# Second attention of a two-block model: a new order of the unit on every engine, and who scales which score pairs

## What is computed

```python
def xattn1(latents, context, Wq, Wk, Wv, Wo, q_norm_w, k_norm_w):
    kv = concatenate([context, latents], axis=1)          # 64 + 256 keys a batch
    q = (latents @ Wq)  # 32 heads of 128
    k, v = kv @ Wk, kv @ Wv                               # 8 key/value heads of 128
    q, k = rms_norm(q, q_norm_w), rms_norm(k, k_norm_w)
    probs = softmax(einsum(q, k) / sqrt(128))             # 4 query heads share a kv head
    return einsum(probs, v) @ Wo
x = x + tanh(g_xattn[1]) * xattn1(layernorm(x), ctx, ...)
```

## Time and profile before

| | us |
|---|---|
| median of 3 runs | 1468.65 (1466.71 to 1475.12) |
| the profiled execution | 1468.23, its span 1466.4 |
| PE busy | 1393.1 (95%) |
| DVE busy | 1056.6 (72%) |
| ACT busy | 799.1 (54%) |
| POOL busy | 464.6 (32%) |
| mean granted TensorE clock | 0.992 of full speed |

### The profile page before, as it was taken

How to read it: one execution, slowest core, us unless ns; L and a number is a source line. 1 busy time by engine, 2 the same in 40 slices (tenths; PEclk the granted TensorE clock), 3 DMA queues, 4 the chain that set the end, 5 groups by cost and what they waited for, 6 DMA issues and landing times.

```text
span 1466.4 us, 24308 instructions
## 1 busy us (share of the span) xinstructions
PE 1393.1 (95%) x7976; PEld 1197.5 (82%) x7976; DVE 1056.6 (72%) x2794; ACT 799.1 (54%) x2210; POOL 464.6 (32%) x591
## 2 busy tenths in 40 slices
PE   4999999999999988999999999999999999999988
PEld 4899999987778877888888888888888888887777
DVE  7777777887514347787787787777787787787775
ACT  4778777773202225565555555555655655555631
POOL 3965555655937421111121111111111211112220
PEclk9999999999999999999999999999999999999999
DMA  5221111212312201001001001001001001010001
GB/s 194 73 72 60 57 70 72 72 58 72 104 42 72 98 1 72 1 1 73 1 1 72 0 1 72 0 1 72 0 1 72 0 1 72 14 42 1 1 8 51
DMA packets 14959, 63.96 MB, mean 44 GB/s; under 512 B 1761, under 2 KB 1761, under 8 KB 10657
## 3 DMA queue, kind: packets, MB, share of 16 engines
q1 hardware_dynamic: 14880, 63.07, 12.3%
HBM read 60.97 MB, written 2.10 MB: 43 GB/s over the span
## 4 chain that ended last, share of the span: by engine, by line
PE 40%; DVE 15%; issue 5%; ACT 4%; DVEq 0%; ACTq 0%
PE psum L57 12%; PE psum L59 11%; PE psum L58 11%; PE psum L1359 2%; PE psum L1453 2%; DVE mx L1044 2%; DVE pT_hi L1017 2%; DVE w1o_lo L1006 1%; DVE pT_lo L1013 1%; DVE p L1059 1%; DVE w1q_lo L1006 1%; ACT pT_hi L1215 1%; DVE dump L1037 1%; DVE oT_lo L1023 1%; DVE v_lo L1074 1%
## 5 line engine op out<-in xcount | busy, mean ns | idle before, releaser
L1292 ACT ACTIVATE p<-psum,nb,rq 128x320 f32<-128x320 f32 x256 | 155.1, 613 | 163.1 <-DVE nb L1048 163.0
L57 PE MATMUL psum<-w1q_hi,xnT_lo 128*128 128x512 f32 x288 | 121.9, 423 | 16.4 <-DVE v_lo L1068 8.6
L981 POOL TENSOR_TENSOR rk<-ssk,rms_eps 128x3 f32<-128x3 f32 x32 | 6.3, 196 | 352.1 <-DVE ssk L1085 352.1
L1013 DVE TENSOR_TENSOR pT_lo<-psum,pT_hi 128x512 fp32r<-128x512 f32 x128 | 88.1, 689 | 40.0 <-ACT pT_hi L1215 38.3
L59 PE MATMUL psum<-w1q_hi,xnT_hi 128*128 128x512 f32 x288 | 114.5, 398 | 0.0
L58 PE MATMUL psum<-w1q_lo,xnT_hi 128*128 128x512 f32 x288 | 113.7, 395 | 0.0
L1044 DVE TENSOR_REDUCE mx<-psum 128x2 f32<-128x640 f32 x128 | 105.0, 820 | 6.5 <-PE psum L59 0.9
L1256 ACT ACTIVATE q_raw<-psum 128x512 f32<-128x512 f32 x64 | 38.2, 597 | 122.7 <-PE psum L59 122.7
L57 PE MATMUL psum<-w1o_hi,oT_lo 128*128 128x512 f32 x256 | 100.5, 393 | 0.0
L58 PE MATMUL psum<-w1o_lo,oT_hi 128*128 128x512 f32 x256 | 100.3, 392 | 0.0
L59 PE MATMUL psum<-w1o_hi,oT_hi 128*128 128x512 f32 x256 | 99.8, 390 | 0.0
(11 more groups left out here) (236 smaller groups left out, 4658.3 us busy)
## 6 DMA issues: line engine op xcount, KB each, us to landing
raw_q<-in_w0q SPq DMA_DIRECT2D x8, 1024.0 KB, 4.9
raw_o<-in_w0o SPq DMA_DIRECT2D x8, 1024.0 KB, 4.8
raw_q<-in_w1q SPq DMA_DIRECT2D x8, 1024.0 KB, 7.5
raw_o<-in_w1o SPq DMA_DIRECT2D x8, 1024.0 KB, 4.8
raw_kv<-in_w_gu SPq DMA_DIRECT2D x10, 512.0 KB, 3.6
raw_gu<-in_w_gu SPq DMA_DIRECT2D x10, 512.0 KB, 3.6
raw_kv<-in_w0kv SPq DMA_DIRECT2D x8, 515.0 KB, 3.3
raw_kv<-in_w1kv SPq DMA_DIRECT2D x8, 512.0 KB, 5.5
```

The costliest lines, as they stand in the source:

```text
L57: pe.matmul(out, w[1], m[0], start=start, stop=False)
L1013: last = dve.tensor_tensor(k.pT[1][:, kt, 2 * hp:2 * hp + 2, :], bank.rearrange("p (h q) -> p h q", h=2), f(k.pT[0][:, kt, 2 * hp:2 * hp + ...
L1292: last = act.activation(k.p1[:, tile, h, :], s_pair(j)[:, h % 2, :], ACT.Exp, bias=k.nb[:, i:i + 1], scale=k.rq[:, i:i + 1], accum_out=k.r ...
```

## The change

All of it is in the second attention and in the first steps of the tail.

- The unit is put in another order on PE, ACT and DVE. Turns 0, 1 and 2 of a unit's p come at the end of the unit itself (around its last scores); turns 3, 4 and 5, p_v and out stay in the next unit, spread between its projections: p_v(0) and turns 3 and 4 behind kv, then half of q's projection, k's transposes, turn 5, the other half, q's first transposes, p_v(1), q's second transposes, and scores and out as before.
- q is projected by pairs of heads instead of by tiles of tokens: 48 matmuls of 256 columns instead of 24 of 512. Its transposes and its split go by pairs of heads too, and score pairs 2 and 3 change places, so that the first two pairs use the first half of q.
- POOL scales the second and the third score pair; DVE the first and the fourth (before: POOL the first, DVE the other three).
- The next group's weight pieces are split elsewhere: o's in batch 1; kv's and q's in batch 3, q's last two low parts in the next group's first unit.
- DVE's list of the 8 groups is written out; PE, ACT and POOL keep the loop.

```diff
-    PAIRS = [(0, 0), (0, 1), (1, 0), (1, 1)]
+    PAIRS = [(0, 0), (1, 0), (0, 1), (1, 1)]
...
+        order = ["t3", "t4", "k", "t5", "q0", "q1", "t0", "t1", "t2"]
...
+    def pieces(g, b):
+
+        return {1: [("o", g, i) for i in range(CONV["o"])],
+                3: [("kv", g + 1, i) for i in range(CONV["kv"])] + [("q", g + 1, i) for i in range(CONV["q"])]}.get(b, [])
...
-                    p_scale(n, 0)
+                    p_scale(n, 1)
+                    p_scale(n, 2)
...
-                if j == 0:
+                if j in (1, 2):
                     return
...
+                    if prev:
+                        t_lo(u, b, 5)
+                    q_squares(n, 0)
+                    if conv:
+                        w_lo(*conv[1])
+                    q_squares(n, 1)
+                    q_lo(n, b, 0)
+                    for c in conv[2:4]:
+                        w_lo(*c)
+                    if prev:
+                        pv_lo(u, b, 1)
+                    q_lo(n, b, 1)
                     row_max(n, 0)
                     row_max(n, 1)
...
                     scale_p(n, 0)
+                    scale_p(n, 1)
+                    row_max(n, 2)
                     if prev:
+                        x_add(u, b, 0)
+                    scale_p(n, 2)
+                    if prev:
+                        x_add(u, b, 1)
+                    t_lo(n, b, 0)
+                    row_max(n, 3)
+                    t_lo(n, b, 1)
...
+                    t_lo(n, b, 2)
                     scale_p(n, 3)
...
-            loop(dve, body, tail)
+            for g in range(NKV):
+                body(g, g == 0, g < NKV - 1)
+            tail(NKV * BATCH)
...
+            def q_proj(n, b, hp):
+                for tile in range(2):
+                    t = 2 * b + tile
+                    for c in range(CH):
+                        last = mm3(pe, y_bank(b, "q", hp)[:, tile * 256:(tile + 1) * 256],
+                                   [w[:, c, t * PART:(t + 1) * PART] for w in k.xnT],
+                                   [w[:, c, hp * 256:(hp + 1) * 256] for w in k.w_q], c == 0, c == CH - 1)
+                last.then_inc(q_full, 1)
...
+                    if prev:
+                        if b % 2 == 0:
+                            pe.wait_ge(kv_split, n + 1)
+                        p_v(u, b, 0)
+                        before = ln_tiles(u)
+                        turn(u, b, 3, late=before[1] if before else False)
+                        turn(u, b, 4)
...
+                    if b % 2 == 0:
+                        pe.wait_ge(cx_split, 2 * g + b // 2 + 1)
+                    else:
+                        pe.wait_ge(kv_split, n + 1)
+                    q_proj(n, b, 0)
                     if prev:
-                        turn(n, b, 4)
-                        turn(n, b, 5)
-                        p_v(n, b, 0)
-                        pe.wait_ge(t_split, 6 * (n - 1) + 5)
+                        pe.wait_ge(t_split, 6 * u + 4)
                     pe.wait_ge(k_scaled, n + 1)
...
+                    if prev:
+                        turn(u, b, 5)
+                        pe.wait_ge(pv_split, 2 * u + 1)
+                    else:
+                        pe.wait_ge(kv_split, n + 1)
+                    q_proj(n, b, 1)
+                    pe.wait_ge(kt_split, n + 1)
+                    q_turn(n, b, 0)
+                    if prev:
+                        p_v(u, b, 1)
+                    q_turn(n, b, 1)
                     scores(n, b, 0)
                     scores(n, b, 1)
...
                     scores(n, b, 2)
                     if prev:
-                        out(n, b, 1)
+                        out(u, b, 1)
+                    turn(n, b, 0)
+                    turn(n, b, 1)
                     scores(n, b, 3)
+                    for i, tile in enumerate(late):
+                        pe.wait_ge(t_split, 6 * n + i + 1)
+                        ln.pe_turn(pe, *tile, ln_bank(b, i))
+                    turn(n, b, 2, late=late[0] if late else False)
 
             def tail(n):
+                u = n - 1
                 ffn1.pe_ag(pe, 0)
+                pe.wait_ge(x_added, 2 * u - 1)
+                p_v(u, 0, 0)
+                turn(u, 0, 3, late=ln_tiles(u)[1])
+                turn(u, 0, 4)
+                ffn1.pe_ag(pe, 1)
                 ffn1.pe_base(pe, 0)
...
```

More of the change, by code:

```diff
@@ L1069, in body @@
                                       ALU.subtract).then_inc(kv_split, 1)
+                    if b == 0 and not first:
+                        w_lo("q", g, 2)
+                        w_lo("q", g, 3)
                     if b % 2 == 0:
@@ L1087, in body @@
                     last.then_inc(ssk_ready, 1)
+                    if prev:
+                        t_lo(u, b, 3)
+                        t_lo(u, b, 4)
+                    dve.wait_ge(rk_ready, n + 1)
+                    for i in range(nk):
+                        last = dve.tensor_scalar(k.k_raw[:, i, :], k.k_raw[:, i, :], k.rk[:, i:i + 1], None, ALU.mult)
+                    last.then_inc(k_scaled, 1)
+                    if prev:
+                        pv_lo(u, b, 0)
                     if not nxt and b >= 2:
@@ new lines, in body @@
+                    if prev:
+                        t_evac(u, b, 5)
+                    if conv:
+                        w_hi(*conv[1])
+                    for late in ln_tiles(n):
+                        ln.act_norm(act, *late)
+                    q_copy(n, b, 1)
+                    q_hi(n, b, 0)
+                    for c in conv[2:4]:
+                        w_hi(*c)
+                    if prev:
+                        pv_evac(u, b, 1)
+                    q_hi(n, b, 1)
+                    exps(n, 0)
@@ L1300, in tail @@
+                    exps(n, 1)
+                    for c in conv[4:]:
+                        w_hi(*c)
+                    exps(n, 2)
+                    t_evac(n, b, 0)
+                    t_evac(n, b, 1)
+                    for i, tile in enumerate(ln_tiles(n)):
+                        ln.act_hi(act, *tile, ln_bank(b, i))
+                    t_evac(n, b, 2)
+                    exps(n, 3)
             def tail(n):
+                u = n - 1
                 ffn1.act_ag(act, 0)
+                pv_evac(u, 0, 0)
@@ L1362, in turn, with p_v @@
                 last.then_inc(t_full, 1)
-            def p_v(n, b, hp, alone=False):
+            def p_v(u, b, hp):
                 pb = (b - 1) % BATCH
-                pe.wait_ge(t_split, 6 * (n - 1) + 3 * (hp + 1))
-                if not alone:
-                    pe.wait_ge(q_copied, 2 * n + hp + 1)
+                pe.wait_ge(t_split, 6 * u + 3 * (hp + 1))
                 for kt in range(2):
@@ L1375, in p_v, with out @@
                 last.then_inc(pv_full, 1)
-            def out(n, b, j):
-                pe.wait_ge(pv_split, 2 * n)
+            def out(u, b, j):
                 for h in range(GH):
+                    if j == 0 and h % 2 == 0:
+                        pe.wait_ge(pv_split, 2 * u + h // 2 + 1)
                     last = mm3(pe, y_bank(b, "d", j)[:, :], [w[:, h, j * PART:(j + 1) * PART] for w in k.oT],
@@ L1382, in out, with q_turn @@
                 last.then_inc(d_full, 1)
+            def q_proj(n, b, hp):
[6 more added lines that the diff above has]
+                last.then_inc(q_full, 1)
+            def q_turn(n, b, hp):
+                pe.wait_ge(q_copied, 2 * n + hp + 1)
+                for hh in range(2):
+                    for tile in range(2):
+                        at = tile * 256 + hh * HD
+                        last = pe.transpose(x_bank(b, "q", hp)[:, (2 * hh + tile) * PART:(2 * hh + tile + 1) * PART],
+                                            k.q_raw[:, hp, at:at + HD], k.ident[:, :])
+                last.then_inc(qt_full, 1)
             def scores(n, b, j):
                 tile, hp = PAIRS[j]
-                if j == 0:
-                    pe.wait_ge(kt_split, n + 1)
-                if hp == 0:
-                    pe.wait_ge(qt_split, 2 * n + tile + 1)
+                if tile == 0:
+                    pe.wait_ge(qt_split, 2 * n + hp + 1)
                 if not (isinstance(n, int) and 4 * n + j < 2):
@@ L1399, in body @@
                     n, prev = BATCH * g + b, not (first and b == 0)
-                    deep = not (first and b < 2)
+                    u, deep = n - 1, not (first and b < 2)
+                    late = ln_tiles(n)
                     if b == 0:
@@ L1690, in pe_hgT @@
         if s == 0:
-            pe.wait_ge(self.free["turned"], 6 * self.units - 1)
+            pe.wait_ge(self.free["turned"], 6 * self.units)
         else:
```

308 lines of the change are left out of this document (100 added, 208 removed).

## The result

The changed kernel takes 1445.62 us by median of 4 runs (1444.20 to 1448.57); the kernel before, beside it, 1468.18. The ratio is 0.9842, with a 95% interval of 0.9812 to 0.9872: 23 us or 1.6% less. I had said 1448.0, between 1432 and 1470, faster with a chance of 0.76. The profiled execution is 1446.38 us with a span of 1444.6, against 1468.23 and 1466.4 of the kernel before.

A forecast was written before the change was run, and what follows sets the result against it. TensorE's order was taken to set the end, its waits being all that can be gained in the second attention's units. The terms -5.5 -11 +5 -3 -5.5 = -20 against 1468.23 gave 1448 us, range 1432 to 1470.

The forecast's parts named there:

- DVE written out, -5.5: DVE's loop in the second attention: five branches each cost TensorE 1.1 us; written out, -5.5 us.
- The reading of the waits: TensorE's weight-load waits over 24 middle units: 33.1 us without v_lo's, 1.38 per unit, all taken as p's six transposes.
- The walk through a unit: One unit in the new order, each wait checked: -0.4 us per unit, -11 us over units 2 to 29.
- rival 3: DVE comes late behind its head, so scores(0) starts 1.2 us late in each unit: +36, 1484; chance 0.11.
- 256 columns, +0.29: q projection: 48 matmuls at 0.120 us instead of 24 at 0.228, +0.29 us a unit.
- POOL's third pair: Scaling moved from DVE to POOL in each unit: worth nothing where DVE isn't last; upper end 0.4 us a unit.
- Start, +5: Units 0 and 1: unit 0 grows from 22 to 29 us, unit 1 falls to about 25.4; +5, between +1 and +9.
- Units 30 and 31, -3: Last two units: from 32.5 and 29.15 us to 30.0 and 28.6, -3 us.
- Tail, -5.5: TensorE's 3.21 us wait for w1q's last piece and 2.4 us of half clock go: -5.5 us.
- The waits only move: Edges with 0.3 us of slack give way, units stay at 27.7 and 25.4: 1459 us; chance 0.22.
- No new wait: No new wait remains: units at 26.5 and 25.0, a start of +3, 1435 us; chance 0.10.
- The ends cost more: Unit 0 at +9, no gain in units 30 and 31, half of the tail's: 1458 to 1466; chance 0.05.

The follow-up runs named there:

- Variants B and C: The changed kernel with POOL scaling the second pair alone: B 1452.68 us; C, with POOL also waiting for DVE's nb of the third pair, 1448.34 us.
- the other run: The changed kernel unchanged, run once more as the reference in the second group of runs: 1446.91 us, ratio 0.9863.

## Why the prediction was right, step by step

**DVE written out, -5.5.** Right: -5.4 alone, and 6.8 in the new order, which I had not added.

**The reading of the waits.** Three readings of the rows were off, and none of them spoilt the sum. Of the 33.1 us of old waits 11.3 are under "issue" and stand neither in the first half of a unit nor at p's transposes. An even unit's matmuls at the prediction's own spacings add up to 22.4 us, so they leave 5.3 of 27.7 and not "some 3"; nothing was worked out from the 3. And unit 1 was called cold, but its clock is 1.00 in the earlier trace rows: its 28.5 us hold 4.4 us of waits at weight loads.

**The walk through a unit.** -11 was forecast for units 2 to 29 beside the branches, -18.9 + 6.8 = -12.1 was measured. Units of 27.1 and 25.1 were forecast, 26.86 and 25.12 measured. Of its terms: the new wait at turn 2, 0.3 forecast, is 0.37. The context's split, 0.15 in even units, is 0.02. The three edges with 0.3 us to spare, for which I had allowed 0.15, held in odd units. There the third score pair waits for ACT's exponentials instead (third row of the waits: 0.33 at the weight load, some 0.2 by the starts of the matmuls). In even units scores(0) starts 0.21 us late (0.29 before). The trace puts this down to "issue"; DVE's split of q, behind both sums of squares, ends 0.13 before the matmul, so I take it to be that. This is rival 3's chain at a sixth of the size at which it would have decided. The -1.38 of old waits is right in sum, though a third of it was read wrongly: the 7.1 us at q's second transposes went, in even units alone, which gained 0.87 us against 0.27 in odd ones, and the 4.2 hardly shrank. What I didn't see is 0.4 at TensorE's branch, five times, or +2. The order of the turns was never undone alone: its share is what is left when the parts that were undone are taken off.

**256 columns, +0.29.** The spacing of 0.12 was right. Alone and in the old order the edit cost 0.13 a unit; what it costs in the new order isn't measured.

**POOL's third pair, "worth nothing where DVE isn't last".** Wrong in its reason, and the one real fault of the argument. I took DVE's busy share and its free 5 us per unit for room; but between the third pair's exponential and the split of turn 0 DVE has only 0.4 to 0.5 us to spare in an odd unit. Two scalings more there cost 0.8 in an odd unit and 0.26 in an even one: 17 us in all by the spans (1461.6 against 1444.6). One costs 0.5 in an odd unit, but only as long as nb is stretched too. It didn't show in the sum, because my walk of the unit had put the scalings on POOL from the start; I had costed the move at nothing beside a walk that needed it. I also wrote that what stands beside POOL's scalings has its first input in PSUM. nb hasn't, and in every odd unit it was stretched from 0.16 to 0.59 (among the even units of the middle unit 14 alone has 0.45, the others 0.16 to 0.18). It was hidden, as Variants B and C show, only by that second scaling.

**Start, +5.** Measured +6.1, and +8.7 in the other run, inside the bounds of +1 to +9. The step that was off is unit 0, 31.4 and 32.9 where I said 29. TensorE's waits in unit 0 of the changed kernel:

```profile
PEld psum L57 <- issue: 6.5, 3, 2.9
PEld psum L1360 <- POOL p L977: 2.1, 1, 2.1
PEld psum L120 <- DVE pT_lo L1017: 1.5, 1, 1.5
PEld psum L1398 <- ACT q_raw L1226: 1.2, 1, 1.2
PEld psum L57 <- DVE qT_lo L1048: 1.2, 1, 1.2
```

By the starts of the matmuls, against unit 0 of before, q's projection starts 2.9 later, of which 2.7 is the wait for the context's split (I had 2). The first score pair comes only 0.1 later than that: for q's split behind the sums of squares I had 2.5, and the 1.2 of the last row are there, but an old wait of 1.9 us at q's transposes, for the split of k, is gone. The third pair is another 1.3 late, behind ACT's exponentials, which I didn't have. The turns and the LayerNorm tiles cost 5.1 more, where I had 2.4: turn 0 waits 2.1 for POOL to scale the second pair, which in my walk was ready ahead of time, and the second LayerNorm tile 1.5 for the split of its bank. So one term was nearly nothing and another twice its size; that their sum came near the forecast is luck. Unit 1 was 25.2, as forecast, or 26.3 in the run where the low clock reached into it.

**Units 30 and 31, -3.** 30.20 and 28.70 against 30.0 and 28.6. The number is right, but not for the reason given alone. Before, unit 30 took 32.5 us at a clock of 0.95. With DVE written out and the old order it took, with the same waits of TensorE,

```profile
1329.49:1360.42 30.93, 28.01 (x165) 23.71 (x164) 22.89 (x72) 17.10 (x44) 6.65 (x13) 1.00 0.00 1
```

So 1.6 of the 2.8 us are the granted clock, which the prediction didn't count here, and 1.2 are the order. To that extent the -3 was luck.

**Tail, -5.5.** Measured -6.5; the 1.0 more I can't place. The base projection, which had waited 3.21 us and run at half clock, in the changed kernel, behind a gate projection:

```profile
1387.31 0.40 PE L57 MATMUL psum<-w1q_hi,xnT_lo 128*128 128x512 f32 x1
1387.55 0.40 PE L58 MATMUL psum<-w1q_lo,xnT_hi 128*128 128x512 f32 x1
```

No wait, and 0.23 us from start to start. The granted clock of the tail is 1.00 where it was 0.95 before. But the half clock didn't always come with the wait: the tail of the kernel before with 256 columns, in the old order and with the same wait of 3.21 us, was

```profile
1403.45:1471.27 67.82, 60.39 (x332) 51.15 (x332) 45.80 (x156) 18.92 (x54) 8.41 (x20) 1.00 0.09 32
```

That is 2.5 us shorter than before, which confirms the 2.4 as its price. In the three profiles of the old order unit 30 had a clock of 0.95, 1.00 and 0.95 and the tail 0.95, 0.95 and 1.00; in those of the new order unit 30 had 1.00 and the tail 0.98 to 1.00 each time. So the new order seems to keep the clock up, but with three profiles of the old one that isn't shown, and the profiles alone overstate the gain of the ends by what the old order loses only sometimes.

**The rivals.** "The waits only move" fell: the waits of the middle without v_lo's went from 33.1 us to 17.6. "No new wait" fell by the row of turn 2. "DVE late behind its head" is there with 0.2 in half of the units, not 1.2 in all. "The ends cost more" fell, though its +9 for unit 0 came true (+9.4); units 30 and 31 and the tail gained what I had forecast.

## What to carry to other kernels

Ask for each engine not how much it idles but what it does between the last input and the next output that the bound engine waits for: two scalings of 0.6 us in that stretch cost 0.8 in an odd unit on an engine that is busy for 72%, and which engine had them decided over 17 of the 23 us. Such a stretch has a slack, so costs on it don't add up: two delays that each cost next to nothing cost 7.5 us together. When edits come together, undo each alone, and a pair of them together: an edit costed at nothing may be the one that keeps the walk of the other true. And an instruction that is delayed on purpose can shorten the kernel, if it got in the way of a small one on a chain.

## What the runs showed of the hardware that I had not expected

- A VectorE product of 128x2 with both inputs in SBUF took 0.59 us instead of 0.16 beside a POOL scaling, and ended with it; with POOL held back, 0.16 again.
- DVE's first instruction behind its loop branch came 2.30 to 2.59 us late in every pass, in the three profiled kernels that keep its loop. On TensorE there is a small one too: 0.39 us at each branch in the new order, nothing to be seen in the old one.
- A wait of 3.21 us on TensorE was followed by half clock in one profile (matmuls of 512 columns 0.43 us apart) and not in another (0.23 apart), with the same work around it.
- The same kernel got a clock of 0.84 in unit 0 in one run and 0.73 in another, with 2.6 us between them over two units. A change in the start of that size needs more than one profile.
